# Reordering the end of a decoder-layer kernel: the last layernorm's statistics, the order of router and delta work, and the engine that scales the last tile

## The reference, cut to what matters

```python
x = _layernorm(x + _L0_attn_ref(x, ...))          # mamba2 block and an MLP of 1792
x = _layernorm(x + _L0_xattn_ref(x, ctx, ...))    # 32 query heads, 8 key/value heads of 128
x = _layernorm(x + _L0_ffn_ref(x, router_w, A, B))

def _L0_ffn_ref(x, router_w, A, B):               # 4 experts, rank 16, top 2
    flat = x.reshape(-1, D)
    logits = flat @ router_w.T
    topk_vals, topk_idx = jax.lax.top_k(logits, 2)
    sparse = jnp.full_like(logits, -jnp.inf).at[rows, topk_idx].set(topk_vals)
    gates = jax.nn.softmax(sparse, axis=-1)
    mid = jnp.einsum('tf,erf->ter', flat, A)
    all_deltas = jnp.einsum('ter,eor->teo', mid, B) * 4.0
    return jnp.einsum('te,teo->to', gates, all_deltas)

def _layernorm(x, axis=-1, eps=1e-05):
    m = jnp.mean(x, axis=axis, keepdims=True)
    v = jnp.var(x, axis=axis, keepdims=True)
    return (x - m) / jnp.sqrt(v + eps)
```

## Time and profile before

| what | value |
|---|---|
| time, median of 3 runs | 1024.9 us (1024.14 to 1027.17) |
| the profiled execution: its time | 1025.79 us |
| the profiled execution: its span | 1024.0 us |
| what lies around the span | 1.79 us |
| mean granted TensorE clock | 0.98 of full |
| PE busy | 973.0 us (95%) |
| DVE busy | 597.0 us (58%) |
| ACT busy | 495.0 us (48%) |
| POOL busy | 411.2 us (40%) |

### The profile page before, as it was taken

The page is one execution under the profiler, slowest core; times in us unless marked ns, Lnnn a source line. Parts: engine busy times, 40 slices in busy tenths (PEclk is TensorE's granted clock), DMA queues, the critical chain, the costliest instruction groups (busy, mean ns, idle before and its releaser), DMA issues.

```text
span 1024.0 us, 15445 instructions
## 1 busy us (share of the span) xinstructions
PE 973.0 (95%) x5010; PEld 806.2 (79%) x5010; DVE 597.0 (58%) x1361; ACT 495.0 (48%) x1380; POOL 411.2 (40%) x341
## 2 busy tenths in 40 slices
PE   4897999999999999899999999999999999999886
PEld 3664677788888888788888888888888888888772
DVE  3879465322212247566667666666666676657865
ACT  4634535122312245654655654655555555555544
POOL 3334646534334353343442442532623523533312
PEclk9999899999999999999999999999999999999995
DMA  6110115101110211011011020020110110100002
GB/s 214 42 42 0 42 42 167 55 7 61 61 61 4 99 62 55 22 42 42 21 41 41 20 82 0 20 82 0 26 77 0 61 41 12 50 0 0 1 1 83
DMA packets 12976, 45.58 MB, mean 45 GB/s; under 512 B 1617, under 2 KB 2257, under 8 KB 9873
## 3 DMA queue, kind: packets, MB, share of 16 engines
q1 hardware_dynamic: 12944, 45.20, 12.7%
HBM read 43.10 MB, written 2.10 MB: 44 GB/s over the span
## 4 chain that ended last, share of the span: by engine, by line
PE 86%; DVE 8%; issue 2%; ACT 2%; POOL 1%; DMA 1%; SPq 0%; ACTq 0%; DVEq 0%
PE bank L377 25%; PE bank L378 24%; PE bank L379 24%; PE bank L651 5%; PE bank L661 3%; DVE cbuf L1634 2%; PE bank L775 1%; PE bank L388 1%; DVE xbc L1650 1%; DVE bst L1810 1%; PE bank L638 1%; DMA res<-in_x 1%; PE bank L741 0%; DVE xn L1592 0%; DVE res L1710 0%
## 5 line engine op out<-in xcount | busy, mean ns | idle before, releaser
L377 PE MATMUL bank<-act_hi,w_hi 128*128 128x512 f32 x560 | 226.3, 404 | 4.2 <-ACT cbuf L875 2.3
L379 PE MATMUL bank<-act_hi,w_lo 128*128 128x512 f32 x560 | 220.3, 393 | 0.0
L378 PE MATMUL bank<-act_lo,w_hi 128*128 128x512 f32 x560 | 220.1, 393 | 0.0
L1503 POOL TENSOR_TENSOR pb<-pb,prec 128x512 f32<-128x512 f32 x64 | 66.7, 1042 | 310.1 <-DVE prec L1944 310.1
L1160 ACT ACTIVATE pb<-pb,nmax 128x128 f32<-128x128 f32 x256 | 99.7, 391 | 78.2 <-DVE nmax L1939 78.2
L377 PEld LDWEIGHTS bank<-act_hi,w_hi 128*128 128x128 f32 x560 | 106.4, 190 | 28.9 <-issue 7.5
L378 PEld LDWEIGHTS bank<-act_lo,w_hi 128*128 128x128 f32 x560 | 106.3, 190 | 23.4 <-issue 2.2
L379 PEld LDWEIGHTS bank<-act_hi,w_lo 128*128 128x128 f32 x560 | 106.1, 189 | 23.0
L377 PE MATMUL bank<-w_hi,ot_hi 128*128 128x512 f32 x256 | 105.0, 410 | 0.8 <-DVE res L1957 0.8
L379 PE MATMUL bank<-w_hi,ot_lo 128*128 128x512 f32 x256 | 100.9, 394 | 0.0
L378 PE MATMUL bank<-w_lo,ot_hi 128*128 128x512 f32 x256 | 100.4, 392 | 0.0
(11 more groups left out here) (193 smaller groups left out, 2105.8 us busy)
## 6 DMA issues: line engine op xcount, KB each, us to landing
raw_a<-in_w_q SPq DMA_DIRECT2D x8, 1024.0 KB, 4.8
raw_b<-in_w_o SPq DMA_DIRECT2D x8, 1024.0 KB, 4.8
raw_a<-in_w_gu SPq DMA_DIRECT2D x7, 1024.0 KB, 5.3
raw_b<-in_w_kv SPq DMA_DIRECT2D x8, 512.0 KB, 3.3
raw_b<-in_w_dn SPq DMA_DIRECT2D x7, 512.0 KB, 3.4
res<-in_x SPq DMA_DIRECT2D x8, 256.0 KB, 6.4
raw_b<-in_ctx_t SPq DMA_DIRECT2D x8, 256.0 KB, 3.6
xre<-in_x SPq DMA_DIRECT2D x2, 1024.0 KB, 6.8
```

What stands on the lines that cost most here:

```text
L377: mm(o, l_hi, r_hi, start=first, stop=False)
L378: mm(o, l_hi, r_lo, start=False, stop=False)
L379: return mm(o, l_lo, r_hi, start=False, stop=last)
L1503: TT(pb[:, jj % 2, :, :], pb[:, jj % 2, :, :], prec[:, jj % 2, :].unsqueeze(2).to_broadcast([P, GH, L]), ALU.mult).then_inc(p_norm, 1)
```

## The change

Four things are changed, all behind slot 3 of the last group.

- **Sums.** `BY_ACT` shrinks to tile 0. Tile 2 still goes bank, ACT copy, POOL add (`BY_POOL = (0, 2)`), but its statistics are now `ln_stats(34)` on DVE, behind a wait for POOL's second add. `dl_stats(1)` and `act_var(1)` are gone.
- **Order of the last tiles and deltas.** The final layernorm goes through the tiles in the order `FIN` = 1, 0, 2, 3, ... instead of 0, 1, 2, ... On DVE `add_delta(1)` and `ln_stats(33)` move ahead of `gates_rank(2)`; in the loop over tiles 4 to 7 `last_mean(b - 1)` moves ahead of `ln_stats(32 + b)`. On PE `dl_step(0)` and `dl_step(1)` move ahead (of `f_norm_t(31)` and `lora_in(7)`), and `mt_step(1)` moves ahead of `dl_step(3)`.
- **Last tile.** Tile 7 is scaled by DVE (`TS`, subtract and multiply, new semaphore `n_last`), not by `last_mean(7)` on DVE and `last_norm(7)` on ACT.
- **Router work later in the slots.** `f_norm_t(25)` moves from slot 4 to slot 5; `f_norm_t(26)`, `(27)` and `(28)` move behind `pt_step` of slots 5, 6 and 7; `d_step(last, 7)` moves ahead of `f_norm_t(29)`. ACT's `x2_evac` calls follow, `ln2_apply(29)` moves behind the last `ot_evac`, and `x2_evac(7)` behind `gate_exp(1)` and `dl_copy(0)`. On DVE `add_out(last, 6)` moves ahead of `ot_rest(last, 7)`.

```diff
-        BY_ACT = (0, 2)
+        BY_ACT = (0,)
+        BY_POOL = (0, 2)
+        FIN = [1, 0, 2, 3, 4, 5, 6, 7]
...
-            for b in range(B):
-                sp_eng.wait_ge(n_x, 33 + b)
+            for b in FIN:
+                sp_eng.wait_ge(*((n_x, 33 + FIN.index(b)) if b < 7 else (n_last, 1)))
                 sp_eng.dma_start(out[b], res[:, b, :]).then_inc(st_out, 16)
...
-            def last_slot(jj, fill):
+            def last_slot(jj, fill, late=()):
...
                 pt_step(last, jj)
+                for step, b in late:
+                    step(b)
                 d_step(last, jj - 1)
...
-            last_slot(4, ((f_norm_t, 24), (f_norm_t, 25)))
-            last_slot(5, ((lora_in, 0), (lora_in, 1), (f_norm_t, 26)))
-            last_slot(6, ((lora_in, 2), (f_norm_t, 27)))
-            last_slot(7, ((lora_in, 3), (f_norm_t, 28)))
+            last_slot(4, ((f_norm_t, 24),))
+            last_slot(5, ((f_norm_t, 25), (lora_in, 0), (lora_in, 1)), ((f_norm_t, 26),))
+            last_slot(6, ((lora_in, 2),), ((f_norm_t, 27),))
+            last_slot(7, ((lora_in, 3),), ((f_norm_t, 28),))
             lora_in(4)
+            d_step(last, 7)
             f_norm_t(29)
-            d_step(last, 7)
             mt_step(0)
...
@@ ACT, the last slots and the tail @@
-            last_slot(4, None, (0, 1))
-            last_slot(5, None, (2,))
-            last_slot(6, 27, (3,))
-            last_slot(7, 28, (4,))
+            last_slot(4, None, (0,))
+            last_slot(5, None, (1,), (2,))
+            last_slot(6, 27, (), (3,))
+            last_slot(7, 28, (), (4,))
+            ln2_apply(29)
+            ln2_apply(30)
             x2_evac(5)
-            ln2_apply(30)
             mt_evac(0)
             x2_evac(6)
             ln2_apply(31)
-            x2_evac(7)
             gate_exp(1)
             dl_copy(0)
+            x2_evac(7)
             dl_stats(0)
             gate_exp(2)
             dl_copy(1)
             mt_evac(1)
             mt_evac(2)
-            dl_stats(1)
-            for b in range(B):
+            for b in FIN[:7]:
                 last_norm(b)
...
@@ POOL, rsqrt @@
+                if i >= 32:
+                    i = 32 + FIN[i - 32]
...
@@ DVE, the tail @@
             gates_mid(1)
+            add_delta(1)
+            ln_stats(33)
             gates_rank(2)
             act_var(0)
             gates_mid(2)
-            add_delta(1)
-            ln_stats(33)
+            last_mean(1)
             last_mean(0)
-            act_var(1)
+            dve.wait_ge(dl_pool, 2)
+            ln_stats(34)
             add_delta(3)
-            last_mean(1)
+            last_mean(2)
             ln_stats(35)
-            last_mean(2)
             for b in range(4, B):
                 add_delta(b)
+                last_mean(b - 1)
                 ln_stats(32 + b)
-                last_mean(b - 1)
-            last_mean(7)
+            dve.wait_ge(n_rstd, 40)
+            TS(res[:, 7, :], res[:, 7, :], mv[:, 39, 0:1], rstd[:, 39:40], ALU.subtract, ALU.mult).then_inc(n_last, 1)
```

More of the change, by code:

```diff
@@ L223, in build_program @@
                                                 sem("a_ssq"))
+        n_last = sem("n_last")
         block = ctx.enter_context(nc.Block())
@@ L249, in dl_freed @@
         def dl_freed(b):
-            if b in BY_ACT:
-                return dl_cp, BY_ACT.index(b) + 1
-            return dl_add, sum(x not in BY_ACT for x in range(b + 1))
+            if b in BY_POOL:
+                return dl_cp, BY_POOL.index(b) + 1
+            return dl_add, sum(x not in BY_POOL for x in range(b + 1))
         def kv_bank(g, n, j):
@@ L804, in _ @@
             lora_in(6)
+            dl_step(0)
             f_norm_t(31)
-            dl_step(0)
+            dl_step(1)
             lora_in(7)
-            dl_step(1)
             dl_step(2)
+            mt_step(1)
             dl_step(3)
-            mt_step(1)
             dl_step(4)
@@ L1238, in last_norm @@
             def last_norm(b):
-                act.wait_ge(n_rstd, 33 + b)
-                act.wait_ge(mr_done, b + 1)
+                act.wait_ge(n_rstd, 33 + FIN.index(b))
+                act.wait_ge(mr_done, FIN.index(b) + 1)
                 A(res[:, b, :], res[:, b, :], ACT.Identity, bias=mr[:, b:b + 1], scale=rstd[:, 32 + b:33 + b])\
@@ L1262, in dl_copy @@
             def dl_copy(k):
-                act.wait_ge(dl_mm, BY_ACT[k] + 1)
-                A(xn[:, k, :], bank[DL_BANK[BY_ACT[k]]][:, :], ACT.Copy).then_inc(dl_cp, 1)
+                act.wait_ge(dl_mm, BY_POOL[k] + 1)
+                A(xn[:, k, :], bank[DL_BANK[BY_POOL[k]]][:, :], ACT.Copy).then_inc(dl_cp, 1)
             def dl_stats(k):
@@ L1282, in _, with last_slot @@
                 slot(last, jj, lead=False, refill=False)
-            def last_slot(jj, apply, tiles):
+            def last_slot(jj, apply, tiles, late=()):
                 if apply is not None:
@@ L1289, in last_slot @@
                 pt_evac(last, jj)
+                for b in late:
+                    x2_evac(b)
                 if jj < 7:
@@ L1293, in last_slot @@
                     gate_exp(0)
-                    ln2_apply(29)
                 ot_evac(last, jj)
-            last_slot(4, None, (0, 1))
-            last_slot(5, None, (2,))
-            last_slot(6, 27, (3,))
-            last_slot(7, 28, (4,))
+            last_slot(4, None, (0,))
[4 more added lines that the diff above has]
+            ln2_apply(30)
             x2_evac(5)
-            ln2_apply(30)
             mt_evac(0)
@@ L1553, in dl_sum @@
                 pool.wait_ge(dl_cp, k + 1)
-                b = BY_ACT[k]
+                b = BY_POOL[k]
                 TT(res[:, b, :], res[:, b, :], xn[:, k, :], ALU.add).then_inc(dl_pool, 1)
@@ L2019, in last_mean @@
             def last_mean(b):
-                dve.wait_ge(n_rstd, 33 + b)
+                dve.wait_ge(n_rstd, 33 + FIN.index(b))
                 if b in BY_ACT:
@@ L2107, in last_slot @@
                     ln_bias(29)
+                add_out(last, jj - 1)
+                if jj == 7:
                     ot_rest(last, 7)
-                add_out(last, jj - 1)
                 if jj > 4 and jj < 7:
```

## The result

The changed kernel takes 1018.4 us in the median of 8 runs (1016.49 to 1020.77) against 1023.45 of 8 runs before (1020.20 to 1027.17). The ratio is 0.9954 with an interval of 0.9935 to 0.9972, about 4.7 us. So it is faster by half a per cent; 1018.5 and "faster" were forecast. The sum came out near although three of its terms did not (the clock, the new gate, the base that the gain was taken off), and the runs show the gain in another place than where the prediction put most of it.

The account below looks back on a forecast made before the run. DVE's 5.52 us wait for ACT's sums of tile 2 was taken to bound the end. Gate 7.0 us sooner (7.0 - 0.8 = 6.2), pace costing 0.25, last tile giving 0.5: 1024.9 - 6.4 = 1018.5, 8-in-10 range 1015.8 to 1021.8.

Parts of the forecast that it names:

- The sum: All terms added over the whole kernel: span 1017.6, 6.4 us less, median 1018.5.
- the clock: PE's granted clock falls to half at 995.1, 7.5 us after the last projection began, as before.
- the new gate: Before delta 3's addition: DVE waits about 1.9 us for POOL's root; the gate opens 7.0 us sooner.
- the base that the gain was taken off: The median of the kernel before, taken as 1024.9 us, less 6.4.
- What bounds the end: Last 65 us: DVE stands 5.52 us for ACT's sums of tile 2, held by an unrelated PE transpose; then 1.80 per tile.
- Slots 4 to 6: PE's 1.90 us wait in slot 4 goes, 0.25 us gained, slot 5 gets transposes back: net nothing.
- The last projection: PE starts the last projection at 987.55 instead of 988.60, a gain of 1.05 us.
- The first rival: The clock stays up through the deltas, each taking 0.90 us: median 1017.7; 10%.
- the third rival: The gate moves instead of going: gate_exp(2) waits for gates_rank(2), DVE's wait grows to about 5.9 us, median 1022.5; 9%.
- the 0.8 of unlisted gaps: Allowance added to the span because the same addition for the kernel before gave 1023.2 against the trace's 1024.0.
- The pace: DVE's last five tiles run at 1.85 us each instead of 1.80, costing 5 x 0.05 = 0.25 us.
- The last tile: One DVE instruction of 0.54 us replaces bias and ACT scaling of 1.10, gaining 0.5 us; store 2.48 as before.

Follow-up runs that it names:

- e2: The changed kernel with tile 2's sums put back on ACT, behind mt_evac(2); median 1019.25 us, ratio 0.9959 to the kernel before.
- e4: The kernel before with slots 4 to 7 and the last projection rearranged, old order behind it; median 1018.89 us, ratio 0.9958.
- e9: The kernel before with only slots 4 to 7 rearranged, last projection and all behind it in old order; median 1026.54 us, ratio 1.0017.
- e5: The changed kernel with last_mean(b-1) behind ln_stats again for tiles 3 to 7; median 1017.53 us, ratio 0.9938 to the kernel before.
- e3: The kernel before with only the last tile's scaling moved to DVE; median 1023.20 us, ratio 1.0004.
- e8: The changed kernel with delta 2 added by DVE straight from the bank and last_mean behind ln_stats; median 1016.81 us, ratio 0.9938 to the kernel before.
- e6: The changed kernel with ACT's copy of delta 2 ahead of gate_exp(2); median 1017.27 us, ratio 0.9928 to the kernel before.
- before_again: The kernel before, unchanged, run and profiled once more; median 1025.08 us, ratio 1.0007.

## Why the prediction was right, point by point

- **What bounds the end.** That DVE paces the last tiles behind one gate was right. What the gate costs was misread: "an ACT wait for an unrelated transpose holds up DVE's last five tiles" is true, but the remedy that counts is the sooner transpose. e2, with the sums still on ACT, has 5.7 of the 6.9 us, and e4, with PE's old order behind the projection as well, 5.8. The prediction's largest term, 7.0 us for the gate, was argued from moving the sums and the deltas; the runs give most of it to the projection's order and the clock.
- **Slots 4 to 6: "Net: nothing".** Right where PE keeps its full clock: e9, which changes the slots alone, adds delta 3 at 51.7, as the first profile of before does (51.75). It missed that in three of the five profiles with PE's 1.90 us gap, half clock for 3.4 us followed it.
- **The last projection.** Forecast 28.6 us after slot 4's scores; it was 28.5. Right.
- **The clock.** "I let it fall as long after the projection as before: 995.1" was the step that failed most. It fell 15 us after the projection began (14.8 to 15.6), in all nine profiles with the new order; with the old one it was 7.5 in two (before, e9) and 13.6 to 13.9 in three. One profile of before was taken for the rule. The first rival had the direction (the clock stays up), at 10%, but not the reason.
- **The new gate.** Forecast: PE brings delta 2 at 1000, ACT and POOL follow, DVE waits 1.9 us for POOL's root. Measured: delta 2 was there by then, the copy waited until 1001.68 for `gate_exp(2)`, hence for `gates_rank(2)` on DVE (the third rival's link, in small), and DVE's wait for the root was 0.19 us, since DVE itself was held for a microsecond by POOL's add. The slow instructions that I didn't have (two times 1.0 us) took back what the faster deltas gave: delta 3 was forecast, with the 0.8 of unlisted gaps, 45.5 us after slot 4's scores, and added at 44.9.
- **The pace.** 1.90, not 1.85: mis-sized by 0.05 per tile, the reason right (e5).
- **The last tile.** 0.5 forecast, 0.52 measured from the root to the end of the scaling. It reached the end of the program because the pace was 1.90: with 1.80 (e3, e5, e8) the store took 0.4 of it back. The prediction had the store at 2.48 in every case.
- **The sum.** Tail 58.6 forecast (1017.6 - 958.97), 58.1 and 58.0 measured. For the median 6.4 us were forecast, 4.7 (0.9954) and 6.0 (0.9941) measured. The profile of before had the longer of its two tails, 65.0; the second had 62.9. A mean over both would have given a smaller gain. That the median was met to 0.1 us is luck: 1024.9, from which the 6.4 were taken, was the median of three runs, 1.5 us above that of eight (1023.45), and the gain was put 1.4 too high (5.05 between the medians). In the sum, deltas that were faster than forecast and DVE instructions that were slower cancelled.

## What to carry to other kernels

A long wait in a profile is the distance to whatever its releaser was itself waiting for: follow it one step further before pricing it, here from DVE to ACT to PE. Where much rests on when TensorE's clock falls, read more than one profile of the same kernel; the times of its runs (1019 to 1028) already say that one isn't enough, and the mean granted clock of each run says it for runs without a profile. Look at what stands in front of TensorE's last dense block: here that block, moved ahead of four transposes with ACT's and DVE's order to match, was worth 0.3% alone. And test the parts of a change apart and together: two of these four (the new order of the last tiles, the new last instruction) gave nothing by themselves, and the one that paid most is not the one that the prediction built on.

## What the runs showed of the hardware that I had not expected

**DVE behind POOL.** A small DVE instruction with two inputs in SBUF that starts beside a POOL `tensor_tensor` of 128x512 (1.26 us) ends only with it: 1.21, 1.23 and, in e6, 1.08 us instead of 0.16 to 0.19. Those with one SBUF input in this stretch (the reduction of 0.19, statistics, additions from a PSUM bank) were not held. The trace of the kernel before had it in one row that I passed over:

```profile
1003.84 1.26 POOL L1555 TENSOR_TENSOR res<-res,xn 128x512 f32<-128x512 f32 x1 [1.70 <-ACT xn L1265]
...
1004.11 1.01 DVE L2023 TENSOR_TENSOR mr<-asum,rstd 128x1 f32<-128x1 f32 x1
```

One column took 1.01 us, to the end of POOL's add. Far ahead of the change the same trace shows it for a large instruction, and where the count of inputs doesn't tell (POOL, then DVE):

```profile
66.95 1.30 POOL L1365 TENSOR_TENSOR em<-em,md 128x512 f32<-128x512 f32 x1 [1.85 <-ACT em L915]
68.39 1.31 POOL L1360 TENSOR_TENSOR md<-dt_sb,cst 128x512 f32<-128x512 f32 x1
```
```profile
67.14 1.66 DVE L1634 SCALAR_TENSOR_TENSOR cbuf<-pre,cw,cbuf 128x512 f32<-128x512 f32 x1
...
68.92 0.81 DVE L1667 TENSOR_SCALAR sp<-sp 128x16 f32<-128x16 f32 x1
```

The first takes 0.75 us when nothing is beside it; here it ends 0.55 us after POOL's, as if it had run only then. The second has one SBUF input and was held all the same, to 0.03 us after POOL's end. So "two inputs" covers what happened in the tail, not every case. The Trainium skill ("GPSIMD Engine Reference", section "8. Key points") says that GpSimd shares its SBUF interfaces with VectorE, with contention for VectorE instructions in a 2-port mode or with two SBUF inputs; the rows agree, and add that here the whole remainder of the POOL instruction was waited for. Which mode the `TENSOR_SCALAR` at 68.92 ran in, no trace here shows.

**Half clock in pieces.** Away from the tail, half clock came and went in stretches of 3.4 us, now and then two in a row. The one in slot 4 cost 1.6 us (from slot 4's scores to slot 5's 9.35 us in before_again, 7.78 in before). Their sum ahead of the change differed between executions of the same kernel, and so did the start of slot 4: 23.9 us and 960.4, 17.1 us and 956.9 for the changed kernel. It is not the only thing that moves it: the kernel before had 13.7 us and 20.5 us of them and began slot 4 at 958.97 and 958.70. That TensorE was busy all the time did not bring the full clock back in the tail: 8.00 of 8 us busy at 0.50 in e9's row above. What decides between the two ways in which the old order lost time, I leave open; the runs here show that the one went with the old slot 4 and the other with the old projection order, not why.
